# A two-layer perceiver kernel: head 0's first key rows and its queries built in SBUF from tripled loads

## The reference, cut to what matters

```
def _L0_xattn_ref(qkv, y):
    q = qkv.reshape(bs * N_HEADS, ch, length)          # 16 heads, ch = 16, length = 512
    k = v = y.reshape(bs * N_HEADS, ch, -1)            # 8192 keys
    scale = 1.0 / math.sqrt(math.sqrt(ch))
    weight = jnp.einsum('bct,bcs->bts', q * scale, k * scale)
    weight = jax.nn.softmax(weight.astype(jnp.float32), axis=-1)
    a = jnp.einsum('bts,bcs->bct', weight, v)
```

## Time and profile before

| | us |
|---|---|
| median of 3 runs (1428.79 to 1431.13) | 1430.67 |
| the profiled execution's own time | 1430.77 |
| its span in the trace | 1429.0 |
| busy PE / DVE / ACT / POOL | 1374.0 / 1151.4 / 940.8 / 138.9 |

### The profile page before, as it was taken

One profiled execution on the slowest core, in us unless ns is written; L12 is line 12 of the kernel. 1 busy time (PEld: TensorE's weight loads), 2 busy tenths in 40 slices (PEclk: granted clock), 3 DMA queues, 4 the chain that ended last, 5 costly groups with the idle time before them and its releaser, 6 DMA issues. The chain is left out here.

```text
span 1429.0 us, 27307 instructions
## 1 busy us (share of the span) xinstructions
PE 1374.0 (96%) x10680; PEld 834.9 (58%) x10680; DVE 1151.4 (81%) x1670; ACT 940.8 (66%) x1764; POOL 138.9 (10%) x171
## 2 busy tenths in 40 slices
PE   3999999999999999999899999999989889999998
PEld 2433333333333333333457999999978664567997
DVE  5999999999999999998487666666658456887665
ACT  1588888888888888889184554555533540786453
POOL 4122221211222222021000000000000000000000
PEclk9999999999999999999999999999999999999999
DMA  7545655465445555445203755445445514203751
GB/s 179 141 104 113 154 127 133 137 155 125 104 113 112 110 125 111 86 65 83 89 1 146 296 197 186 176 176 187 166 179 248 236 65 171 67 1 93 203 188 38
DMA packets 63569, 192.54 MB, mean 135 GB/s; under 512 B 32872, under 2 KB 33296, under 8 KB 51280
## 3 DMA queue, kind: packets, MB, share of 16 engines
q1 hardware_dynamic: 63264, 190.80, 46.4%
q10 hardware_dynamic: 192, 0.20, 0.1%
HBM read 165.72 MB, written 21.83 MB: 131 GB/s over the span
## 5 line engine op out<-in xcount | busy, mean ns | idle before, releaser
L530 DVE TENSOR_REDUCE pm<-bank 128x1 f32<-128x1024 f32 x512 | 621.1, 1221 | 15.8 <-PE bank L611 10.0
L589 ACT ACTIVATE probs<-bank 128x512 f32<-128x512 f32 x1024 | 554.7, 598 | 98.2 <-PE bank L630 96.9
L611 PE MATMUL bank<-kst,qst 48*128 48x512 f32 x1024 | 370.8, 453 | 21.9 <-DMA qst<-qsplit 20.2
L630 PE MATMUL bank<-qst,kst 52*128 52x512 f32 (+1 forms) x1024 | 372.9, 448 | 1.3 <-DVE pm L530 0.8
L647 PE MATMUL bank<-probs,vext 128*32 128x256 f32 x3968 | 316.7, 391 | 0.0
L630 PEld LDWEIGHTS bank<-qst,kst 52*128 52x128 f32 (+1 forms) x1024 | 153.1, 185 | 210.2 <-ACT probs L589 182.0
L1378 PE MATMUL bank<-e_xhi,e_hi 128*128 128x256 f32 (+1 forms) x768 | 217.4, 283 | 0.5 <-DVE e_xlo L1438 0.5
L1378 PE MATMUL bank<-e_xhi,e_lo 128*128 128x256 f32 (+1 forms) x768 | 217.2, 283 | 0.0
L1378 PE MATMUL bank<-e_xlo,e_hi 128*128 128x256 f32 (+1 forms) x768 | 217.2, 283 | 0.0
L647 PEld LDWEIGHTS bank<-probs,vext 128*32 128x32 f32 x3968 | 78.1, 108 | 181.4 <-ACT probs L589 91.5
L611 PEld LDWEIGHTS bank<-kst,qst 48*128 48x128 f32 x1024 | 149.5, 187 | 29.9 <-DMA qst<-qsplit 20.2
(11 more groups left out here) (220 smaller groups left out, 1520.3 us busy)
## 6 DMA issues: line engine op xcount, KB each, us to landing
raw<-wall SPq DMA_DIRECT2D x43, 1536.0 KB, 6.6
kst<-kscratch SPq DMA_DIRECT2D x192, 128.0 KB, 4.4
kscratch<-ksplit SPq DMA_DIRECT2D x15, 1024.0 KB, 4.6
kraw<-ctx_rows SPq DMA_DIRECT2D x16, 512.0 KB, 6.2
vraw<-ctx_vt SPq DMA_DIRECT2D x16, 512.0 KB, 7.1
ctxT<-ctxT SPq DMA_DIRECT2D x8, 1024.0 KB, 11.6
nat<-ctx_chunks SPq DMA_DIRECT2D x6, 1024.0 KB, 21.7
weights<-wscratch SPq DMA_DIRECT2D x16, 256.0 KB, 3.4
```

The lines of the kernel that those rows point to most:

```text
L530: nc.vector.tensor_reduce(pm[:, h % 2, r % 4, c:c + 1], bank[:, 2 * (r % 2):2 * (r % 2) + 2, :], AX.XY, ALU.max).then_inc(pre_reduced, 1)
L589: nc.scalar.activation(probs[:, (XST * k + n) % PR, :], bank[:, S_BANK[k][n], :], ACT.Exp, scale=XSCALE).then_inc(probs_ready, 1)
L611: ins = nc.tensor.matmul(bank[:, 2 * (r % 2) + j, :], qst[64 * j:64 * j + KR, h, tt * P:tt * P + P], kst[64 * j:64 * j + KR, h % 2, c * 51 ...
L630: nc.tensor.matmul(bank[:, S_BANK[k][n], :], kst[64 * j:64 * j + rows, h % 2, m * P:m * P + P], qst[64 * j:64 * j + rows, h, :], start=Tru ...
```

## The change

Head 0's first key half and its queries no longer go through DRAM.

- **Loads.** SP loads each of the 16 channels three times, into 48 neighbouring partitions: `xstack` (tokens) and `krep` (keys; columns 0-511, then 512-2047). So rows 3c, 3c+1 and 3c+2 belong to channel c: high, low, high for keys. DVE first sets partitions 32-63 and 96-127 of both tiles to zero, and the loads wait for that.
- **Split in place.** DVE makes two masks from the identity, `is_rest` (1 where the row holds a low part) and `sign` (1 or -1). ACT makes `khigh` = rounded `krep` x sign, and `krep` x is_rest; POOL adds them into `kst`, in four pieces of 512 columns, counted by `first_keys`. DVE normalizes `xstack` (its statistics beside those of `X`) and writes head 0's `qst` itself.
- **PE.** Eight matmuls of 128 columns on the identity (`FIRST_WARM`) run as soon as the square root is done; then `pre(0, 0, 1)` waits for the queries and the first piece of keys.
- **Moved.** `xn` and `qsplit` of the other heads are now made by POOL, between `split(0)` and `split(1)`. The four `marks` transfers stand ahead of the store of head 0's split keys, and after `first_keys` has come to 4, since POOL's additions write all 128 partitions. Head 0's split keys are stored in one transfer, and only the second half is read back, to every third partition.

```
+FIRST_COLS = 512
+FIRST_WARM = 8
...
+            sp.wait_ge(dve_step.sem, 1)
+            for j in range(2):
+                sp.dma_start(xstack[64 * j:64 * j + KR, :], x[0:XC].unsqueeze(1).to_broadcast([XC, 3, D])).then_inc(x_loaded, 16)
+            keys = ctx_rows[0].rearrange("(c s) n -> c (s n)", c=XC)
+            for n, (lo, hi) in enumerate(((0, FIRST_COLS), (FIRST_COLS, XK // 2))):
+                sp.wait_ge(dve_step.sem, n + 1)
+                for j in range(2):
+                    sp.dma_start(krep[64 * j:64 * j + KR, lo:hi],
+                                 keys[:, j * XK + lo:j * XK + hi].unsqueeze(1).to_broadcast([XC, 3, hi - lo])).then_inc(stack_lo[n], 16)
             load_raw(0)
             load_raw(1)
-            sp.wait_ge(split_step, 1)
-            sp.dma_start(kscratch[0, 0], ksplit[:, 0, :].bitcast(F32)).then_inc(first_high_stored, 16)
-            sp.wait_ge(split_step, 2)
-            sp.dma_start(kscratch[0, 1], ksplit[:, 1, :].bitcast(F32)).then_inc(split_stored, 16)
-            sp.wait_ge(first_high_stored, 16)
-            load_rows(0, 0, K_ROWS[0])
-            load_rows(0, 0, K_ROWS[2])
+            load_v(0)
+            sp.wait_ge(const_set, 2)
+            sp.wait_ge(first_keys, 4)
+            for b in range(2):
+                for j in range(2):
+                    row = 64 * j + KR
+                    sp.dma_start(kst[row:row + 4, b, :].bitcast(F32),
+                                 marks[:, :, :].rearrange("k s n -> k (s n)").bitcast(F32)).then_inc(negmax_stacked, 16)
+            store_split(0)
             sp.wait_ge(split_stored, 16)
-            load_rows(0, 0, K_ROWS[1])
-            sp.wait_ge(stack_lo[0], 192)
             load_stack(0, 1)
-            sp.wait_ge(qsplit_ready, 4)
...
-                if h == 0:
-                    load_v(0)
-                    sp.wait_ge(const_set, 2)
-                    for b in range(2):
-                        for j in range(2):
-                            row = 64 * j + KR
-                            sp.dma_start(kst[row:row + 4, b, :].bitcast(F32),
-                                         marks[:, :, :].rearrange("k s n -> k (s n)").bitcast(F32)).then_inc(negmax_stacked, 16)
                 if h < XH - 1:
                     load_stack(h + 1, 0)
+                    if h == 0:
+                        sp.wait_ge(queries_ready, 1 + 2 * TA)
...
-            split(0)
-            pool.wait_ge(qsplit_ready, 4)
-            split(1)
             nc.gpsimd.memset(marks[:, :, :].bitcast(F32), 1.0).then_inc(const_set, 1)
             pool.wait_ge(const_set, 1)
             nc.gpsimd.memset(marks[0:2, 1, :].bitcast(F32), 0.0).then_inc(const_set, 1)
+            for c in range(4):
+                cols = slice(512 * c, 512 * c + 512)
+                pool.wait_ge(split_step, c + 1)
+                nc.gpsimd.tensor_tensor(kst[:, 0, cols], krep[:, cols], khigh[:, cols].bitcast(F32), ALU.add).then_inc(first_keys, 1)
+            split(0)
+            pool.wait_ge(queries_ready, 1)
+            for a in range(TA):
+                nc.gpsimd.tensor_scalar(xn[:, a, :], X[:, a, :], fmv[:, a, 0:1], frstd[:, a, :],
+                                        ALU.subtract, ALU.mult).then_inc(g.xn_ready, 1)
+                pool.wait_ge(g.xn_ready, a + 1)
+                nc.gpsimd.tensor_copy(qsplit[:, 0, a], xn[:, a, :]).then_inc(queries_ready, 1)
+                pool.wait_ge(queries_ready, 2 * a + 2)
+                nc.gpsimd.tensor_tensor(qsplit[:, 1, a], xn[:, a, :], qsplit[:, 0, a].bitcast(F32), ALU.subtract).then_inc(queries_ready, 1)
+            split(1)
...
-            dve.wait_ge(x_loaded, 16)
-            norm_dve(g, dve, 0, link)
-            for a in range(TA):
-                dve.wait_ge(g.xn_ready, a + 1)
-                nc.vector.tensor_copy(qsplit[:, 0, a], xn[:, a, :]).then_inc(qsplit_ready, 1)
-                dve.wait_ge(qsplit_ready, 2 * a + 1)
-                nc.vector.tensor_tensor(qsplit[:, 1, a], xn[:, a, :], qsplit[:, 0, a].bitcast(F32), ALU.subtract).then_inc(qsplit_ready, 1)
+            assert dve_step.n == 0
+            for j in range(2):
+                nc.vector.memset(xstack[64 * j + 32:64 * j + 64, :], 0.0)
+                ins = nc.vector.memset(krep[64 * j + 32:64 * j + 64, 0:FIRST_COLS], 0.0)
+            link(ins)
+            for j in range(2):
+                ins = nc.vector.memset(krep[64 * j + 32:64 * j + 64, FIRST_COLS:], 0.0)
+            link(ins)
+            dve.wait_ge(g.ident_ready, 2)
+            halves = ident[:, :].rearrange("p (j r) -> p j r", j=2)
+            for n in range(2):
+                ins = nc.vector.tensor_reduce(is_rest[:, n:n + 1], halves[:, :, 1 + n:KR:3], AX.XY, ALU.add)
+            link(ins)
+            link(nc.vector.tensor_scalar(sign[:, :], is_rest[:, :], -2.0, 1.0, ALU.mult, ALU.add))
+            signs.append(dve_step.n)
+            dve.wait_ge(x_loaded, 48)
+            rows = [X[:, 0, :], X[:, 1, :], xstack[:, :]]
+            for a in range(3):
+                ins = nc.vector.bn_stats(fstats[:, a, :], rows[a])
+            link(ins)
+            for a in range(3):
+                ins = nc.vector.bn_aggr(fmv[:, a, :], fstats[:, a, :])
+            link(ins)
+            nc.vector.tensor_scalar(fvar[:, :, :], fmv[:, :, 1:2], EPS, None, ALU.add).then_inc(g.var_ready, 1)
+            dve.wait_ge(g.std_ready, 1)
+            link(nc.vector.reciprocal(frstd[:, :, :], fstd[:, :, :]))
+            link(nc.vector.tensor_tensor(fstd[:, :, :], frstd[:, :, :], frstd[:, :, :], ALU.mult))
+            link(nc.vector.scalar_tensor_tensor(out=fstd[:, :, :], in0=fstd[:, :, :], scalar=-0.5, in1=fvar[:, :, :],
+                                                op0=ALU.mult, op1=ALU.mult))
+            link(nc.vector.scalar_tensor_tensor(out=frstd[:, :, :], in0=fstd[:, :, :], scalar=1.5, in1=frstd[:, :, :],
+                                                op0=ALU.add, op1=ALU.mult))
+            link(nc.vector.tensor_scalar(xnstack[:, :], xstack[:, :], fmv[:, 2, 0:1], frstd[:, 2, :], ALU.subtract, ALU.mult))
+            link(nc.vector.tensor_scalar(qhigh[:, :], xnstack[:, :], sign[:, 1:2], None, ALU.mult))
+            nc.vector.scalar_tensor_tensor(out=qst[:, 0, :], in0=xnstack[:, :], scalar=is_rest[:, 1:2], in1=qhigh[:, :].bitcast(F32),
+                                           op0=ALU.mult, op1=ALU.add).then_inc(queries_ready, 1)
...
+            act.wait_ge(dve_step.sem, signs[0])
+            act.wait_ge(g.var_ready, 1)
+            nc.scalar.activation(fstd[:, :, :], fvar[:, :, :], ACT.Sqrt).then_inc(g.std_ready, 1)
+            for c in range(4):
+                cols = slice(512 * c, 512 * c + 512)
+                if c < 2:
+                    act.wait_ge(stack_lo[c], 32)
+                nc.scalar.activation(khigh[:, cols], krep[:, cols], ACT.Copy, scale=sign[:, 0:1])
+                nc.scalar.activation(krep[:, cols], krep[:, cols], ACT.Copy, scale=is_rest[:, 0:1]).then_inc(split_step, 1)
             act.wait_ge(kraw_loaded[0], 16)
             nc.scalar.copy(ksplit[:, 0, :], kraw[:, 0, :]).then_inc(split_step, 1)
-            act.wait_ge(g.var_ready, 1)
-            nc.scalar.activation(g.std[:, :, :], g.var[:, :, :], ACT.Sqrt).then_inc(g.std_ready, 1)
-            for row, part in Q_ROWS:
-                act.wait_ge(qsplit_ready, part + 1)
-                for j in range(2):
-                    nc.scalar.dma_start(qst[64 * j + row:64 * j + row + XC, 0, :].bitcast(F32),
-                                        qsplit[0:XC, part, 0, :].bitcast(F32)).then_inc(stack_lo[0], 16)
...
+                    if k == 0:
+                        if r == 0:
+                            pe.wait_ge(queries_ready, 1)
+                        if tt == 0:
+                            pe.wait_ge(first_keys, r // 4 + 1)
...
+            pe.wait_ge(g.std_ready, 1)
+            for i in range(FIRST_WARM):
+                nc.tensor.matmul(bank[:, 4, 0:P], ident[:, :], ident[:, :], start=True, stop=True)
```

More of the change, by code:

```diff
@@ L245, in cross_attention_0 @@
     marks = at(0, "marks", [4, 2, XK // 2], F32R)
+    krep = at(16, "krep", [P, XK // 2])
+    khigh = at(24, "khigh", [P, XK // 2], F32R)
+    xstack = at(96, "xstack", [P, D])
+    xnstack = at(98, "xnstack", [P, D])
+    qhigh = at(100, "qhigh", [P, D], F32R)
+    fstats = at(102, "fstats", [P, 3, 6])
+    fmv = at(102.125, "fmv", [P, 3, 2])
+    fvar = at(102.25, "fvar", [P, 3, 1])
+    fstd = at(102.375, "fstd", [P, 3, 1])
+    frstd = at(102.5, "frstd", [P, 3, 1])
+    is_rest = at(102.625, "is_rest", [P, 2])
+    sign = at(102.75, "sign", [P, 2])
     nscratch = nc.dram_tensor("nscratch", [XN, P, 32], F32, kind="Internal").ap()
@@ L254, in cross_attention_0 @@
     split_stored = sem("split_stored")
-    first_high_stored = sem("first_high_stored")
+    first_keys = sem("first_keys")
     stack_lo = [sem("stack_lo0"), sem("stack_lo1")]
@@ L259, in cross_attention_0 @@
     v_ready = sem("v_ready")
```

(22 more changed lines are left out.)

## The result

The changed kernel takes 1446.53 us (median of 4 runs, 1443.15 to 1447.69) against 1430.48 before, with a fourth run of that kernel: ratio 1.0107, 95% interval 1.0092 to 1.0121. The medians lie 16.1 us apart, 15.3 by the ratio. It is slower, and outside the stated range, which ended at 1436.0. The ratios leave out slow executions, of which there was one, in experiment 6 (1640.51 us at a mean granted clock of 0.75). The profiled execution took 1443.15 us with a span of 1441.4, so 12.4 us of the loss can be read in its trace (before: 1430.77 and 1429.0).

What follows compares the result with a forecast made beforehand. The prediction took the compute chain and SP's queue, meeting at score(0, 0), to bound the start, with DVE and PE full behind. Sum: 1430.77 + 0.5 (later score(0, 0)) + 1.0 (clock) = 1432.3 us; range 1427.5 to 1436.0.

Steps and rivals of the forecast that it cites:

- Two chains: At score(0, 0): the compute chain and SP's queue meet there, and a gain needs both to come earlier.
- the head start: At the kernel's start: first matmul at about 13, 7 us earlier, turning into a wait ahead of pre(1, 7).
- SP's queue: Ahead of score(0, 0): maximum's transfer goes at 43.4, giving score(0, 0) at 48.2 against 47.70, 0.5 us later.
- term one: C: Start of SP's queue: the time head 0's store has landed, taken as 28.0.
- the price of the marks: SP's queue ahead of head 0's store: 256 KB at 36 GB/s, 7.1 us.
- T4: End of POOL's four additions, when the last piece of head 0's first keys is ready: 16.2.
- the store's share behind them: Head 0's store on the engines that carried the marks: 1 MB at 376 GB/s, 2.8 us.
- rounding up: Landing of head 0's store: 27.6 taken as 28.0, to cover issue time.
- term two: the clock: Behind PE's wait ahead of pre(1, 7): two rounds at half speed cost 1.1 us, taken as 1.0.
- The queue slips further: Rival, chance 0.22: head 0's store lands at 30 or more, score(0, 0) at 50 to 52, time 1434.3 to 1437.
- The two that gave a gain: Rivals: head start passes through whole (0.07, 1423.5 to 1425); marks do not hold the store (0.16, 1427.3 to 1429.3).
- the four cases: The forecast (0.55, 1429.8 to 1434.8) and three rivals: whole head start 0.07, marks not holding 0.16, queue slipping 0.22.

Runs made afterwards that it cites:

- experiment 6: Changed kernel with marks in eight transfers, two of them behind the first keys, and step 0's maximum issued ahead of head 1's read-back: 1430.29 us (0.9983).
- experiment 1: Changed kernel with the four marks transfers moved back behind head 1's store: 1446.33 us (1.0105).
- 4: Changed kernel with the marks in eight transfers, only two of which wait for the first keys: 1437.79 us (1.0045).
- 5: Changed kernel with marks in eight transfers, two behind the first keys, plus 26 pairs of readerless matmuls ahead of score(0, 0): 1430.52 us (1.0009).
- 2: Changed kernel with 26 pairs of readerless matmuls ahead of pre(1, 0) and 25 ahead of score(0, 0): 1439.55 us (1.0068).
- 8: Changed kernel with marks split, step 0's maximum first, and readerless pairs beside step 0's rounds from the first one on: 1427.07 us (0.9986).
- 10: Changed kernel with marks split, step 0's maximum first, later heads' loads spread, POOL's constants early, readerless pairs from the first round: 1432.23 us (1.0026).
- 12: Changed kernel with marks split, maximum first, readerless pairs from the first round, POOL's constants early, ten readerless pairs ahead of score(1, 0): 1427.96 us (0.9999).
- 11: Changed kernel with marks split, step 0's maximum first, readerless pairs from the first round, POOL's constants ahead of the first keys: 1426.83 us (0.9978).
- 7: Kernel before the change with only step 0's maximum issued ahead of head 1's read-back: 1432.09 us (1.0024).

## Why the prediction was wrong

**Right: the mechanism.** It is slower for the reason named. Two chains meet at `score(0, 0)`; the first matmul at 13.5 (said: 13); the head start becomes a wait; SP's queue is last; the granted clock falls behind the gap. From the landing of head 0's store to `score(0, 0)` I had summed 20.2 us; it was 52.83 less 32.53, 20.3. The parts of it: read-back 6.3 (said 6.5), POOL 3.5 (3.5), head 1's store landed 8.4 after the first (8.8), the queries' first issue 11.8 after it (11.6).

**Wrong, term one: C, the landing of head 0's store, 28.0 said, 32.5 measured; most of it is the price of the marks.** 1.4 us of it are T4, 17.6 instead of 16.2. The groups after show the prices ahead of T4:

```profile
L472 POOL TENSOR_TENSOR kst<-krep,khigh 128x512 fp32r<-128x512 f32 x4 | 5.0, 1271 | 5.8 <-ACT krep L638 5.8
L637 ACT ACTIVATE khigh<-krep,sign 128x512 fp32r<-128x512 f32 x4 | 2.8, 711 | 1.4 <-DMA krep<-ctx_rows 1.4
L543 DVE MEMSET krep<- 32x1536 f32 x2 | 2.7, 1338 | 0.7 <-DVE krep L540 0.4 <-issue 0.4
L539 DVE MEMSET xstack<- 32x512 f32 x2 | 1.0, 485 | 1.1 <-PEq L1935 0.9
```

The memset is near the estimate (485 and 1338 ns, said 450 and 1360), and the 0.6 us that the prediction had as its other figure for 512 elements was too much. A pass with a scale per partition on ACT took 0.71 us and not 0.6, and ACT waited 1.4 us for the larger key load, which I had not priced.

The other 3.1 us lie between T4 and the landing: 14.9 measured, 11.8 said.

| us | said | measured |
|---|---|---|
| T4 to the marks' first packet | 1 | 1.5 |
| the marks' 256 KB | 7.1 | 10.6 |
| the store's share behind them | 2.8 | 2.6 |
| to the landing | 0.5 | 0.2 |
| rounding up | 0.4 | |

So the term that failed is the marks' 7.1 us, from the 36 GB/s of the earlier trace rows. The stretch 31.6 to 34.3 holds the starts of six of the marks' packets, each counted whole, and not other traffic, as the prediction has it. From first to last packet the marks took 8.0 us in the kernel before (29.84 to 37.82), 33 GB/s. So the row read rightly would have given 8.0 us, and the same transfers took 2.6 us longer after the change. Why, no run separates; in experiment 1, where they go out at 32, they took 10.3. SP's long issues, 5.64 for the marks and 2.49 for the store, are not what held the landing: the store was issued by 25.9, and the end of its packets waited for the marks until 29.7.

The Trainium skill (SBUF — State Buffer, Door 1: The DMA port swizzle) puts one port at about 27 GB/s. The trace after agrees within a tenth, at 25 GB/s. The prediction had worked out 9.7 us from that figure, as an estimate, and then summed by its row.

**Wrong, term two: the clock, 1.0 said, 6.7 measured.** I took two rounds at half clock and a round's loss of 0.57, both from the start of the kernel, where the rounds hold no scores. Behind `score(0, 0)` three rounds take 1.7 us, and the five behind them, which hold products with the values too, 2.16 to 2.20 instead of 1.24, a loss of 0.92 each. PE's modelled busy time is 18.00 of 18 us there, and DVE waits for it 0.94 us in a round. And it lasted 20.5 us (50.3 to 70.8), not two rounds: nothing in my rows said how long the low clock stays. The earlier trace rows shows 3.4 us of it behind a gap of 3.44 us, and I carried that length over to another kind of work. Experiments 4 and 5 show the term alone: 1437.79 against 1430.52.

What the profile was to show came in part: the gap (4.9 us, said 4 to 7) and the store of head 1 (36.3, said 30 or later), but the maximum's first transfer at 48.0, said 42 to 45, and `score(0, 0)` at 52.8, said 46.5 to 50.

**The rivals.** "The queue slips further" had the right place and the right sign, with a chance of 0.22 and a price up to 1437. The two that gave a gain had nothing for them: the marks did hold the store. None of the four cases priced a clock that stays low for longer than four rounds.

**Still open.** The median lies 3.4 us above the profiled execution, and the mean granted clocks of the other three (0.985, 0.982, 0.981; the profiled one has 0.985) fall with their times; that those executions lose more to a longer low stretch is a reading of these three numbers, since they have no trace. The spread between executions in 2, 8, 10 and 12 is open too, and so is why some gaps lower the clock and others of like length do not.

## What to carry to other kernels

A head start is worth what the last chain at the first meeting point lets through: list everything that an in-order queue issues ahead of the item waited for, and when it lands, before building the faster start. Where an engine's wait is new, price the clock behind it by rounds of the work that follows, and for longer than the gap; here gaps of 1.4 to 6.2 us among the scores cost 6 to 10 us in the traces of the changed kernel and of 4, 6 and 11, while gaps of 1.2 to 1.6 us in 2, 7 and 10 left the clock full. Readerless matmuls in the gap, or an order that has no gap, took the loss back. Read a rate from the first to the last packet of a transfer, not from a stretch that cuts packets. Transfers to or from four partitions belong where nothing is behind them on the queue, in as few bytes as possible.

## What the runs showed of the hardware

- 256 KB from four partitions to four took 10.6 us after the change (25 GB/s), 10.3 in experiment 1 and 8.0 in the kernel before. SP's issues of the four transfers took 5.64, 7.11 and 3.40 us together; after the change the shortest of them took 0.62 and the longest 2.52.
- After gaps of 4.9, 14.3 and 6.2 us the granted clock stayed at half for 20.5 us here and for 37.5 and 30.7 in experiments 1 and 4, although PE's modelled busy time is 18.00 of 18 us from 53 to 71. A stretch with no scores in it (the rounds of the first step at half clock, 16.2 to 23.0) came back after 6.8, and so did the rounds behind the 6.16 us gap in the changed kernel (36.7 to 43.5). The length of the gap alone does not tell: behind 1.4 us in experiment 6 the clock fell, behind 1.6 us in 10 it did not.
- The second pass of DVE's queries (L569, one input, 512 columns) took 1.44 us, its like beside it 0.55; POOL's addition ran from 11.13 to 12.40 meanwhile, and the pass ended 0.28 us after it. No run separates the two.
- POOL's `xn` (L476, two scalars per partition, 512 columns) took 2.08 us each, a cast of the same size 0.61. It cost nothing in the changed kernel, where POOL waited for the store anyway, and held head 1's store in experiment 1.
- Sixteen rows written to every third partition landed 2.9 to 3.2 us after issue, against 2.9 to 5.1 for sixteen neighbouring ones in the earlier trace rows, where a store and the values were issued right behind them; so the spreading alone is not shown.
